# A hybrid block on one core: retention and feed-forward of two layers as one pipeline of eight units

## What is computed

```python
def _forward(x, ...):                       # 2 layers, 16 heads of 8 channels, D_FFN 512
    for i in range(N_LAYERS):
        ln_x = layer_norm(x, ln1_g[i], ln1_b[i])
        p = ln_x @ proj_w[i] + proj_b[i]
        q, k, v, xo = jnp.split(p, 4, axis=-1)
        scores = jnp.einsum('bhld,bhmd->bhlm', q, k) * D[None]     # decay, causal
        ret = jnp.einsum('bhlm,bhmd->bhld', scores, v)
        ret = ret * jax.nn.silu(xo)
        x = x + ret @ reto_w[i] + reto_b[i]
        h = layer_norm(x, ln2_g[i], ln2_b[i])
        x = x + jax.nn.gelu(h @ ffn1_w[i] + ffn1_b[i], approximate=False) @ ffn2_w[i] + ffn2_b[i]
    return layer_norm(x, lnf_g, lnf_b)
x = x + _forward(_layernorm(x), ...)        # the part that is changed
x = x + moe(_layernorm(x))                  # 8 experts, 2 for each token
x = x + attention(_layernorm(x))
x = x + moe(_layernorm(x))
```

## Time and profile before

| | us |
|---|---|
| median of 3 runs | 881.59 (880.51 to 881.97) |
| profiled execution, its own time | 881.72 |
| its span, first to last instruction | 879.9 |
| start to the first tile's values (two norms of the input) | 0 to 38.5 |
| retention, layer 0 | 38.5 to 122.4 |
| feed-forward, layer 0 | 122.4 to 168.6 |
| retention, layer 1 | 168.6 to 252.5 |
| feed-forward, layer 1, until its third result is read | 252.5 to 287.0 |
| rest of leave and route until the first scatter | 287.0 to 301.3 |
| scatters to the row table | 301.3 to 343.9 |
| experts, attention, experts | 344 to 880 |

### The profile page before, as it was taken

One profiled execution on the slowest core, in us unless ns is written; L12 is line 12 of the kernel. 1 busy time (PEld: TensorE's weight loads), 2 busy tenths in 40 slices (PEclk: granted clock), 3 DMA queues, 4 the chain that ended last, 5 costly groups with the idle time before them and its releaser, 6 DMA issues.

```text
span 879.9 us, 19404 instructions
## 1 busy us (share of the span) xinstructions
PE 647.0 (74%) x6492; PEld 446.0 (51%) x6492; DVE 628.8 (71%) x1935; ACT 338.0 (38%) x581; POOL 289.8 (33%) x554
## 2 busy tenths in 40 slices
PE   2597888777888311999925788898888972499990
PEld 0254546444556211999923244444444432499990
DVE  6887935787947982888854788677678735388874
ACT  1423143434244311444414055565564561244440
POOL 1223441113464474455522001110512222355551
PEclk9999989999999655999966599999999995699995
DMA  9301189821120011656534421322312000255554
GB/s 208 124 2 50 62 151 181 119 88 39 68 67 1 26 52 51 171 165 168 165 96 127 103 57 30 85 50 56 102 50 52 11 17 16 79 167 160 166 151 149
DMA packets 102627, 81.01 MB, mean 92 GB/s; under 512 B 8381, under 2 KB 92797, under 8 KB 102365
## 3 DMA queue, kind: packets, MB, share of 16 engines
q1 hardware_dynamic: 97744, 70.19, 32.5%
q0 software_dynamic: 4544, 9.38, 3.1%
q10 hardware_dynamic: 240, 0.20, 0.1%
HBM read 54.56 MB, written 23.20 MB: 88 GB/s over the span
## 4 chain that ended last, share of the span: by engine, by line
PE 52%; DVE 21%; issue 9%; POOL 6%; ACT 5%; DMA 5%; SPq 1%; DVEq 0%; ACTq 0%; POOLq 0%
PE PC L1982 8%; PE PA L1972 6%; PE PB L1972 6%; DVE rmax L1327 4%; POOL rows_dram L739 4%; PE P L2063 4%; PE PC L1931 3%; PE PA L2023 3%; PE PA L2021 3%; DVE pm L954 2%; PE PA L1843 2%; PE PA L1920 2%; PE PC L1866 2%; PE PC L2046 2%; PE PB L1920 2%
## 5 line engine op out<-in xcount | busy, mean ns | idle before, releaser
L1327 DVE TENSOR_REDUCE rmax<-PA 128x1 f32<-128x512 f32 (+3 forms) x256 | 120.2, 489 | 49.2 <-PE PA L2023 42.3
L751 POOL DMA_INDIRECT outs_dram<-va,ids x78 | 81.3, 1042 | 93.0 <-DVE va L1266 89.2
L739 POOL DMA_INDIRECT rows_dram<-va,idx x64 | 63.1, 986 | 79.8 <-DVE va L1195 61.1
L1982 PE MATMUL PC<-ffn_w,pm 128*128 128x128 f32 x624 | 86.9, 282 | 1.3 <-DMA ffn_w<-in_w 1.2
L2023 PE MATMUL PA<-kst,qst 96*128 96x512 bf16 (+3 forms) x256 | 83.2, 329 | 0.0
L2021 PE MATMUL PA<-mqb,idb 128*128 128x128 bf16 x256 | 59.9, 235 | 25.4 <-DVE rmax L1327 18.5
L1982 PEld LDWEIGHTS PC<-ffn_w,pm 128*128 128x128 f32 x624 | 75.8, 192 | 2.4 <-DMA ffn_w<-in_w 1.9
L1600 ACT ACTIVATE kv_b<-P 128x256 f16<-128x256 f16 x78 | 29.9, 384 | 112.6 <-PE P L1961 112.6
L1256 DVE SCALAR_TENSOR_TENSOR pm<-PB,invb,decay 128x512 f32<-128x512 f32 x78 | 58.5, 750 | 19.6 <-ACT decay L1608 12.8
L2021 PEld LDWEIGHTS PA<-mqb,idb 128*128 128x128 bf16 x256 | 25.2, 98 | 87.9 <-DVE rmax L1327 48.8
L1972 PE MATMUL PA<-kv_b,pm 128*128 128x128 f16 x936 | 67.6, 224 | 0.0
(11 more groups left out here) (239 smaller groups left out, 1444.4 us busy)
## 6 DMA issues: line engine op xcount, KB each, us to landing
ffn_w<-in_w SPq DMA_DIRECT2D x78, 256.0 KB
rows_dram<-wall SPq DMA_DIRECT2D x1, 8385.0 KB, 51.1
X<-in_w SPq DMA_DIRECT2D x32, 256.0 KB, 2.9
proj_w<-rows_dram SPq DMA_DIRECT2D x78, 65.0 KB, 2.1
qst<-parts_dram SPq DMA_DIRECT2D x48, 96.0 KB
kst<-parts_dram SPq DMA_DIRECT2D x48, 96.0 KB
parts_dram<-qkp SPq DMA_DIRECT2D x16, 256.0 KB, 2.6
X<-in_x SPq DMA_DIRECT2D x8, 256.0 KB, 5.0
```

The lines of the kernel that those rows point to most:

```text
L739: nc.gpsimd.indirect_dma_start(out=rows_dram, out_offset=bass.IndirectOffsetOnAxis(ap=idx[:, t, r:r + 1], axis=0), in_=xrow[:, t, :], in_o ...
L751: nc.gpsimd.indirect_dma_start(out=outs_dram, out_offset=bass.IndirectOffsetOnAxis(ap=ids[:, k % YB:k % YB + 1], axis=0), in_=ysb[:, k % Y ...
L1327: nc.vector.tensor_reduce(rmax[:, i, h % HG:h % HG + 1], PA[:, n % 2, 0:(i + 1) * P], AX_X, ALU.max).then_inc(pair_sb[n % 2], 1)
L1982: ins = mm(PC[:, k % 2, 0:D], eT[:, k % 2, f, :], w2b[k % WB2][:, f, :], start=f == 0, stop=f == FB - 1)
```

## The change

Retention and feed-forward of both layers become one loop on each engine. A unit is one sequence in one layer: units 0 to 3 are layer 0, 4 to 7 layer 1, and tile t of 32 belongs to unit n = t // 4, with u = t % 4. In unit n's tiles PE also does the feed-forward of unit n - 2 (up of two blocks at u = 0 and two at u = 1, down at u = 3), the turn, queries and keys of unit n + 1 (u = 2) and the turn of unit n - 1 for its feed-forward (u = 3). Up and down no longer use PA, PB and PC but the two banks of the ring, and hT moves to a buffer of qst. `norm_twice` makes both normalizations of the input from one set of sums, for one sequence at a time: sequence 0 at the start, the others on DVE behind tiles 0, 3 and 5. The norm of a unit's input in layer 1 is made of sums on DVE, factors on POOL and `normalize` on ACT. The largest values of the experts are taken behind tiles 7 to 14, the weights are written behind tiles 18 to 25, one each. `leave(0)` stands behind tile 30. `pad_rows` is issued before the experts' loads, const, decay and one sequence of x are loaded by ACT's queue, and the router's comparison of four tiles is two instructions instead of eight.

The diff, cut to its core:

```diff
+    def front(c):
+        return [("turn", *ln_in(c)), ("q", c), ("k", c)]
+        return [("turn", LNC, s), ("q", UNITS + s), ("k", UNITS + s), ("v", s)]
+    plan = front(0)
+    for n in range(UNITS + 2):
+        if n < UNITS:
+            plan += [("xo", n)]
+        if n >= 2:
+            plan += [("up", n - 2, f) for f in range(FB)]
+        if n + 1 < UNITS:
+            plan += front(n + 1)
+        if n == UNITS:
+            plan += route(0, 0)
+        if n == UNITS + 1:
+            plan += [("count", 0, 0)]
+        if n >= 2:
+            plan += [("down", n - 2)]
+        if 1 <= n <= UNITS:
+            plan += [("turn", *ln_up(n - 1))]
+    for s in range(1, SEQ):
+        plan += route(0, s) + [("count", 0, s)]
...
+            sp.dma_start(X[:, 0:TPS, :], x_t[:, 0:TPS, :]).then_inc(in_x[0], 16)
...
+            for s in (2, 3):
+                sp.dma_start(X[:, TPS * s:TPS * s + TPS, :], x_t[:, TPS * s:TPS * s + TPS, :]).then_inc(in_x[s], 16)
+            sp.dma_start(reto_w[:, :, :], a_reto_w.rearrange("l d n -> d l n")).then_inc(in_reto, 16)
+            sp.dma_start(reto_b[:, :, :], a_reto_b.partition_broadcast(P)).then_inc(in_reto, 16)
             sp.wait_ge(filled, 2)
...
-                    sp.wait_ge(x_free, 1)
+                    sp.wait_ge(xn_ready, SEQ)
...
+            pad_rows()
             for e in range(2 * E):
                 expert_in(e)
...
+            for t in range(LAST):
+                n, u = divmod(t, TPS)
+                decay_k(t)
+                if u == 0:
+                    if n == 0:
+                        pool.wait_ge(in_reto, in_reto_n)
+                    add_reto(n)
+                    if n == UNITS - 1:
+                        add_shift(0)
+                if u == 1:
+                    if SEQ <= n + 1 < UNITS:
+                        norm_factors(STAT[ln_in(n + 1)])
+                    if n == 2:
                         pool.wait_ge(in_ffn, in_ffn_n)
+                    if n >= 2:
+                        add_ffn2(n - 2)
+                if u == 2 and n >= 1:
+                    norm_factors(STAT[ln_up(n - 1)])
+            norm_factors(STAT[(LNM1, 0)])
+            add_ffn2(UNITS - 2)
+            add_shift(1)
...
+            def norm_twice(s):
+                for k in range(TPS):
+                    ins = nc.vector.bn_stats(st6[:, k, :], X[:, TPS * s + k, :])
                 link(ins)
...
+                nc.vector.tensor_scalar(rs[:, 0, 0:TPS], mv[:, 0:TPS, 1], EPS, None, ALU.add)
+                link(nc.vector.tensor_scalar(rs[:, 0, TPS:2 * TPS], mv[:, 0:TPS, 1], 1.0 + EPS, EPS * EPS,
+                                             ALU.mult, ALU.add))
+                y = inverse_roots(2 * TPS)
+                for out, o in ((xn, TPS), (R, 0)):
+                    for k in range(TPS):
+                        t = TPS * s + k
+                        ins = nc.vector.tensor_scalar(out[:, t, :], X[:, t, :], mv[:, k, 0:1], y[:, o + k:o + k + 1],
+                                                      ALU.subtract, ALU.mult)
+                ins.then_inc(xn_ready, 1)
...
+                for t in range(LAST + 2):
+                    n, u = divmod(t, TPS)
+                    if t < LAST:
                         keys_values(t)
...
+                    if t >= 2:
                         update_state(t - 2)
...
+                    if u == 0 and n >= 3:
+                        add_ffn(n - 3)
+                    if t < LAST:
+                        if u == 3 and n + 1 < UNITS:
+                            decay_q(n + 1)
                         decay_scores(t, 0)
                     if t >= 2:
                         add_out(t - 2)
...
+                    if t < LAST:
                         decay_scores(t, 1)
                     if t >= 2:
...
+                    if u == 0 and 3 <= n < SEQ + 3:
+                        row_sums(R, n - 3)
+                        means(*ln_in(n + 1))
+                    if t in (0, 3, 5):
+                        s = (0, 3, 5).index(t) + 1
+                        dve.wait_ge(in_x[s], 16)
+                        if s == SEQ - 1:
+                            dve.wait_ge(stack_fill, 2 * 16)
+                        norm_twice(s)
...
+                    if E - 1 <= t < 2 * E - 1:
+                        largest_weight(t - E + 1)
+                    if t == 2 * E + 1:
                         weight_scales()
...
+                    if 2 * E + 2 <= t < 3 * E + 2:
+                        low_weight(t - 2 * E - 2)
+                    if t == LAST - 2:
+                        leave(0)
...
+            def add_ffn(c):
+                k = RING[("down", c)]
+                dve.wait_ge(ring_ps, k + 1)
+                dve.wait_ge(ffn2_added, c + 1)
+                nc.vector.tensor_tensor(R[:, r, :], ring_bank[k % 2][:, :].rearrange("p (k n) -> p k n", k=TPS),
+                                        R[:, r, :], ALU.add).then_inc(freed("down", c), 1)
+                wait_ring(dve, "down", c)
...
             def leave_and_route():
-                leave(0)
+                mean_factors(STAT[ln_up(UNITS - 1)])
                 leave(1)
                 route(0, 0)
+                add_ffn(UNITS - 2)
                 leave(2)
                 choose_slots(0, 0)
+                add_ffn(UNITS - 1)
                 route(0, 1)
                 choose_slots(0, 1)
                 leave(3)
...
-            def compare(m, k):
+            def compare(m):
                 for o, op in ((cgt_[m], ALU.is_gt), (cge_[m], ALU.is_ge)):
-                    ins = nc.vector.tensor_tensor(o[:, k, :, :], bc(lg[:, k, :], [P, E, E], 1),
-                                                  bc(lg[:, k, :], [P, E, E], 2), op)
+                    ins = nc.vector.tensor_tensor(o, bc(lg[:, :, :], [P, TPS, E, E], 2),
+                                                  bc(lg[:, :, :], [P, TPS, E, E], 3), op)
                 link(ins)
...
+                for n in range(UNITS + 2):
+                    if n < UNITS:
+                        gate_input(n)
+                    if n == 2:
+                        act.wait_ge(in_ffn, in_ffn_n)
+                    if n >= 2:
+                        gelu(n - 2, 0)
+                        gelu(n - 2, 1)
+                    weights(TPS * n)
+                    if n >= 2:
+                        gelu(n - 2, 2)
+                        gelu(n - 2, 3)
+                    weights(TPS * n + 1)
+                    if n + 1 < UNITS:
+                        if n + 1 >= SEQ:
+                            normalize(*ln_in(n + 1))
+                        turn_queries_keys(n + 1)
+                    weights(TPS * n + 2)
+                    if n == UNITS:
+                        normalize(LNM1, 0)
+                        logits(0, 0)
+                    if 1 <= n <= UNITS:
+                        normalize(*ln_up(n - 1))
+                        plain_turn(*ln_up(n - 1))
+                    weights(TPS * n + 3)
...
+            x_t = a_x.rearrange("(t p) d -> p t d", p=P)
+            act.dma_start(const[:, :], a_const).then_inc(in_const, 16)
+            act.dma_start(X[:, TPS:2 * TPS, :], x_t[:, TPS:2 * TPS, :]).then_inc(in_x[1], 16)
+            act.dma_start(decay[:, :, :], a_decay.rearrange("p (h n) -> p h n", h=H)).then_inc(in_decay, 16)
...
+                def up(c, first, end):
+                    wait_ring(pe, "turn", *ln_up(c))
+                    x = xT[:, xt_buffer(*ln_up(c)), :]
+                    for f in range(first, end):
+                        mm(ring("up", c, f), ffn1_w[:, c // SEQ, f * P:(f + 1) * P], x, start=True,
+                           stop=True).then_inc(ring_ps, 1)
+                def down(c):
+                    wait_ring(pe, "up", c, FB - 2)
+                    wait_ring(pe, "up", c, FB - 1)
+                    bank = ring("down", c)
+                    for k in range(TPS):
+                        for f in range(FB):
+                            ins = mm(bank[:, k * D:(k + 1) * D], hT[:, c % 2, f, k * P:(k + 1) * P],
+                                     ffn2_w[:, c // SEQ, f, :], start=f == 0, stop=f == FB - 1)
+                    ins.then_inc(ring_ps, 1)
...
+                for t in range(LAST + 2):
+                    n, u = divmod(t, TPS)
+                    if t < LAST:
                         keys_values(t)
                         scores(t)
...
+                        if u == 0:
+                            gate_input(n)
...
+                    if t == 2 * TPS:
+                        pe.wait_ge(in_ffn, in_ffn_n)
+                    if u < 2 and n >= 2:
+                        up(n - 2, 2 * u, 2 * u + 2)
+                    if u == 2 and n + 1 < UNITS:
+                        plain_turn(*ln_in(n + 1))
+                    if u == 3 and n >= 2:
+                        down(n - 2)
+                    if 1 <= t < LAST + 1:
                         retain(t - 1)
...
+                    if u == 2 and n + 1 < UNITS:
```

(9 more changed lines are left out.)

570 lines of the change are left out of this document (204 added, 366 removed).

## The result

| | before | after |
|---|---|---|
| median of the runs | 881.05 (880.21 to 881.97, 4 runs) | 899.89 (899.06 to 900.9, 4 runs) |
| profiled execution, its span | 881.72, 879.9 | 899.06, 897.3 |
| first decay of scores | 38.8 | 23.0 |
| decay of tile 8 | 78.8 | 83.2 |
| first scatter | 301.28 | 313.63 |

The ratio is 1.0214 (95% interval 1.0196 to 1.0232): 18.8 us slower, and outside the range of 863 to 895. Two thirds of it, 12.4 us, are there at the first scatter.

The account below looks back on a forecast made before the run. It took retention as bound by the circle between PE and DVE, with DVE half idle in the feed-forward. First scatter 3.8 later, less 1.5 for the comparison, net +2.3 on 881.7: 884.0; range 863 to 895.

Parts of the forecast that it names:

- first decay: Start: one combined norm of sequence 0 brings the first decay of scores to about 23.5 instead of 38.83.
- tile 8: Start of tile 8 at 81.5 against 80.7 before; early start and norms between tiles cancel; bounds 79 and 84.
- end of tile 31: From tile 8: 144.1 us of PE work, 39.4 of waits and 7 of clock, ending at 272.0.
- from there to the first scatter: Tail of closing steps, mean factors, leave(1), route, add_ffn, leave(2) and the way to the scatter: 33.1 us.
- the rest, against before: Behind the first scatter and in the attention, the shorter comparison saves twice more, 1.5 us.
- the weights: DVE's waits at low weights for ACT's high weights: 4.4 at tiles 18 and 22, 2.5 at 19 and 23, together 13.8.
- The clock: Tiles 8 to 31: PE's granted clock of 0.93 to 0.96 costs 7 us over the 24 tiles.
- two closing steps: Tail, behind tile 31: the first term of the 33.1 us to the first scatter, put at 5.7.
- the three norms: `norm_twice` on DVE behind tiles 0, 3 and 5 stops the circle of PE and DVE for 17.4 us.
- Rival 1: Start: the row table's fill holds back the experts' loads, everything waits 9 us, total 893; chance 0.10.
- Rivals 2 and 3: Tiles 8 to 31: full clock with waits kept, 877, chance 0.20; weights' waits hidden and clock kept, 863, chance 0.20.
- The drain of 1.4 us a switch: ACT's table switches between gelu and silu: the skill's drain could delay high weights at tiles 20 and 24, 1.4 in all.

Follow-up runs that it names:

- e1: The change with ACT's high weights of u = 2 and u = 3 moved earlier, ahead of normalize and turn; ratio 0.9979 to the kernel before, median 880.5 us.
- e3: The change with leave(0) moved from behind tile 30 into tile 31, ahead of gate(30); ratio 1.0134 to the kernel before, median 893.6 us.
- e11: The kernel before with only the router's comparison cut from eight instructions to two; ratio 0.9993, median 880.5 us.
- e10: e9 with the fill of the row table issued behind the first two experts' loads; ratio 0.9818 to the kernel before, median 863.4 us.
- e9: The change with the edits of e1 (weight behind normalize), e3, e4 and e7 together; ratio 0.9833 to the kernel before, median 865.6 us.
- e7: The change with the norms of sequences 1 to 3 moved ahead of the first tile; ratio 1.0142 to the kernel before, median 891.2 us.
- e8: The change with the fill of the row table back behind the first eight experts' loads; ratio 1.0450 to the kernel before, median 918.3 us.
- e12: e10 with PE's up and down of a tile behind retain instead of in front; ratio 0.9721 to the kernel before, median 857.6 us.
- e4: The change with POOL's three additions of lnf to X moved from the tail into tiles 29 to 31; ratio 1.0163 to the kernel before, median 897.2 us.

## Why the prediction was wrong

By its own steps:

| step | forecast | measured |
|---|---|---|
| first decay | 23.5 | 23.0 |
| tile 8 | 81.5 | 83.2 |
| end of tile 31 | 272.0 | 272.4 |
| from there to the first scatter | 33.1 | 41.2 |
| the rest, against before | -1.5 | +5.1 |

The forecast for the profiled execution was 884.0, and it took 899.06: 15.1 us more, of which 0.4 up to the end of tile 31, 8.1 in the tail and 6.6 behind the first scatter.

1. **Up to tile 31 the sum held within half a microsecond, in part by luck.** The waits were sized well: the weights 13.8 forecast and 15.0 measured (e1 gave 14.3 back), leave(0) 7.2 and 6.7, all waits of tiles 8 to 31 together 39.4, where PE was idle for 39.6 us of 189.2. The clock was sized too small. PE's work in a unit at a granted clock of 1.00 is 24.89 us (unit 3); in units 4 to 6 it is 83.6, so 8.9 us are clock in these three alone, where 7 was meant for all six. The granted clock from tile 8 to 31 was 0.93, as forecast, but by the forecast's own conversion (5.9 us of 83.9 at 0.93) that is 13 us and not 7. Too small a clock was made up for by work that had not been done yet: the forecast put all of unit 7, 22.1 us with its down, before the end of tile 31, and PE had done 17.3 of it. Windows of unit 3 and unit 7, with the columns of the earlier trace rows:

```profile
109.48:138.29 28.81, 24.89 (x242) 15.23 (x242) 21.73 (x47) 14.24 (x23) 11.77 (x43) 1.00 0.17 55
...
248.13:272.40 24.27, 17.28 (x162) 10.38 (x163) 20.29 (x65) 6.58 (x11) 10.27 (x32) 0.90 0.09 18
```

2. **The tail is the step that failed.** The term "two closing steps" was put at 5.7, for which the forecast gives no row, and took 12.0. PE's down of unit 5 was counted inside tile 31, but it ran from 270.39 to 275.98, behind the hole of leave(0) and in front of the retain that DVE waited for; and nothing in the forecast shows that the four ups of unit 6, which PE also does in the closing steps, were counted. The down was slow as well (5.59 at a clock of 0.65, 3.74 at 1.00 in e3). The stop of DVE beside POOL's additions in leave(2), 3.1, was in no term either. Against these, leave was counted 0.8 too long, twice: the price of 7.85 from the earlier trace rows held such a stop beside POOL's additions too, which I did not see. In the kernel before, an instruction that takes 0.17 elsewhere takes 0.90 and ends 0.03 us behind POOL's additions; without such a stop leave takes 7.05 (288.28 to 295.33).

```profile
266.57 0.90 DVE L841 TENSOR_SCALAR rs<-mv 128x4 f32<-128x4 f32 x1
...
262.50 4.94 POOL L726 TENSOR_TENSOR X<-X,lnf 128x512 f32<-128x512 f32 x4
```

3. **Behind the first scatter** I took 1.5 off for the comparison, which e11 can neither show nor exclude, and 5.1 came on top. The instructions there are nearly the same. PE was busy for 430.2 us at a granted clock of 0.84 in the change and for 426.9 at 0.85 in the kernel before, so 3.3 of the 5.1 are the same 4524 matmul records at a lower clock. The kernels that contain the change run this part in 577.8 to 583.7 us, the two without it in 578.6 and 578.4: a part of the 5.1 is a spread between executions. PE's busy time in it goes along, from 425.2 in e10 to 430.5 in e9 (577.8 and 582.5). What sets the clock there stays open.
4. **A gain was missed at the start.** I put the three norms at 17.4 us on the path where they stand, and did not ask what they would cost elsewhere. In front of the first tile they delay the first decay by 6.7 (e7), as DVE waits there for 9 us. That wait was in my own sum: keys 9.5 us behind the norm. I read it as delay and not as room.
5. **The rivals.** Rival 1 did not happen in the change: the first largest value waited for nothing, at 81.53. Its wait is real, and shows as soon as the start is faster (e7, 4.8 us). What I did not see is the other side of that edit: the fill had to move, as behind the experts it makes the first scatter 22 us later (e8). Rivals 2 and 3, full clock and hidden weights, are what e1 made in part: 14.3 us at the first scatter of the 20.8 that the forecast held for them together, with the clock at 1.00 in units 5 and 6 but at 0.91 in unit 4. By the ratios of the medians e1 gave 2.4%, 21 us; what that has above the 14.3 of the first scatter lies outside the part that the edit changes, so the nearness to 20.8 is luck.
6. **The table loads** of ACT are 17 in the whole program against 9 before, so 8 more and not 14. The drain of 1.4 us a switch that the forecast allowed for does not show: where ACT waits for nothing else, its next instruction starts 0.01 to 0.02 us behind the end of the load.

So what the pipeline could have gained went, in the order of size, into the weights' waits and the clock behind them (14 us at the first scatter, e1), norms between tiles (8 at tile 8 in e7, of which 5 were left at the first scatter there and 10 in e9), feed-forward blocks in front of retain (5 to 7, e12), leave(0) (3, e3) and POOL's additions (2, e4), the last two from tile 28 or 31 to the first scatter. With all of them undone the same pipeline has its first scatter at 277.2, 24 us before the kernel before.

## What to carry to other kernels

When stages are merged, write for each engine what it waits for at the new places of every instruction, and put work where that engine is idle anyway (norms into the wait for the first queries) and behind the instruction that the other engine waits for (up and down behind retain). Count the closing steps of a pipeline on every engine, not on the one that was the bound in the middle. In this kernel a wait on PE was paid again in clock behind it (unit 6 in e1, the down behind leave(0) in e3), so the waits to take out first are those just ahead of much PE work. And a price that is read from one row should be checked against a second instance of the same block.

## What the runs showed of the hardware

- DVE's small instructions on SBUF (0.16 us) take 1.19 to 1.20 when they stand beside a POOL addition of 1.25 that reads SBUF: three beside three additions, one beside one (e4). DVE's decays, which read PSUM and SBUF, kept their 1.21 to 1.23 beside the additions that e4 moved into the tiles. The Trainium skill says so: "SBUF — State Buffer", section "Who interferes with whom", has a DVE instruction with two SBUF inputs contend with a GpSimd instruction that reads SBUF, and calls the ports that they share an exclusive lock. The trace agrees, with 1.03 us of wait a time: DVE's first long instruction ends at 300.75, POOL's addition beside it at 300.73.
- A transfer of 4 KB issued behind 8.4 MB on the same queue landed after 37.0 us in e8, 18.6 before and 11.6 in e11 (the order of the kernel before), and after 1.4 in the change, where the fill was long through.
- The granted clock fell to 0.87 and 0.90 in the units with and behind the waits at the weights and stayed at 1.00 in units 5 and 6 of e1 with the same instructions. PE had done 24.90 us of work in 30.60 there. In the change it was 0.65 behind 6.74 us without work, and 1.00 for the same down in e3. It also differs between executions of the same instructions: 0.89 in the change and 0.85 in e3 from 170 to 250 us.
